# Time mixing by one level of Strassen's multiplication, with weight quarters fetched from memory

## The chip, the cores and the metric

The kernel runs on one core of one Trainium2 chip. The metric is the device time of one execution in microseconds (us). TensorE is called PE below (PEld is its weight load), VectorE DVE, ScalarE ACT, GpSimd POOL, SyncE SP. SP and ACT issue the DMA transfers.

## The reference

Four stages, each with x added back, on x of B = 128 rows, 64 channels and T = 1024 steps:

```
x1 = x  + einsum('bct,bcd->bdt', x, W[condition])         # mixes channels, weights by row
x2 = x1 + conv(x1, kernel 1), up to a length per row      # state-space filter along t
x3 = x2 + x2 @ weight.T + bias + scale * low-rank(x2)     # mixes time steps, 1024 x 1024
out = x3 + conv(x3, kernel 3), up to a length per row     # state-space filter along t
```

The third line, "time mixing", is what the change is about: `base = einsum('bsi,oi->bso', x, weight) + bias`, and `delta`, through 16 ranks of the row's adapter. It is applied to each channel's time axis.

## The kernel before

Time is cut in NBLK = 8 blocks of 128 steps, which lie on the partitions; channels in NG = 16 groups of HG = 4. Products in 16-bit are made from two halves: a value is split in a high part (rounded to f16, by ACT) and a low part (the rest, by DVE), and three matmuls (high x high, high x low, low x high) take the place of one. So `x2_split_hi` (L1017) and `x2_split_lo` (L1477) make x2h and x2l, and likewise for x1 (L1013, L1465), the state-space tables (`table_hi` L1031, `table_lo` L1444), their bases (`bases_hi` L1048, `bases_lo` L1450) and x3.

Stage 0 (`stage0`) loads x, mixes channels on PE (L618), and writes x1 to memory as `x1_scratch`. Beside it the time-mixing weights are turned on PE (`turn_lot`, 8 transposes for each of 8 output blocks) and split into `w2t`, which holds them all; `lot_ready` on DVE prepares each row block and adds the identity for the residual. Small tables go to memory with `store_tab`, filters with `store_k`.

Then PE runs `body(g)` for each group: `stage2(g)`, the time mixing of the group's 4 channels at once (512 columns); then, in an order written out by hand, the filter before the mixing for the next group (`states(0, g+1, k)`, `near1`, `far1`) and the filter behind it for this one (`states(1, g, k)`, `near3`, `far3`; L784 and L797). `stage2` begins with the low-rank sums (L737) into bank 7, then for each output block o makes 24 matmuls (L745) and 3 for the low-rank term (`delta`, L753):

```python
for k in range(NBLK):
    for q, (part, xx) in enumerate(products):
        nc.tensor.matmul(ps[:, 4 + o % 3, :], w2t[:, o, part, k, :], xx[:, :, k, :], ...)
```

DVE scales the low-rank sums (L1499) and ACT and DVE split them (L1072, L1502). As each block o ends, ACT makes its x3 high part straight from the bank (L1079), DVE reads the bank again (L1515) and makes the low part (L1509); between blocks both handle the bases and tables. After stage 2 they split the states (`state_hi` L1055, `state_lo` L1457), select the first filter's sums (`take_conv1`, L1472) and split x2.

The output of channel h goes from the banks to `outt[:, h]` (ACT, L1110, counted by c3_out). SP turns x3 (`turn_x3`, L418), POOL adds its two parts (L531, past_summed) and scales them (L534, past_ready) in `past_of`; DVE selects between the two (L1557, c3_past); SP stores it (L448, out_stored). Behind each select DVE makes a low part of x1 for the group after the next (L1465). POOL also makes the tables (`make_tables`, L507 to L521, 7 operations, twice a group): it starts them when the group's four selects are done.

All engines run their own instructions in order and wait for each other's semaphores (`wait_ge`).

## Time and profile before

| | |
|---|---|
| runs before | 1693.88, 1693.52, 1689.08 us; median 1693.52 |
| the profiled execution | 1686.25 us |
| its span, first to last instruction | 1684.4 us |
| mean granted PE clock | 0.978 of full |
| PE, DVE, ACT, POOL busy | 93%, 61%, 31%, 49% |

The rows below are from the profiled execution, times in us unless marked ns, counted from the start of its span. "Idle before" names what ended the idle time. Matmuls overlap, so a matmul's own length (379 ns for 512 columns) is more than the distance to the next one; the chain of waits shows the distances. The granted clock is 1.00 at 2.4 GHz and 0.50 at 1.2 GHz.

### The profile page before, as it was taken

What the parts mean: (1) busy time and instruction counts of PE and PEld (TensorE: products, weight loads), DVE (VectorE), ACT (ScalarE), POOL (GpSimd) and SP (SyncE); (2) the same over time, 40 slices, a digit from 0 to 9 for tenths busy, and PEclk for the clock granted to TensorE, in tenths of its full rate; (3) what the DMA queues carried; (4) which work ended last, traced back from release to release, by engine and by line L of the source; (5) the groups of instructions that cost most, each with busy time, mean ns of one, the idle gap of its engine ahead of it and who ended that gap; (6) DMA issues with size and microseconds to landing.
All of it is one profiled execution on the core that took longest, in us unless ns stands there. A gap on an engine that the chain in (4) does not pass through costs nothing.

```text
span 1684.4 us, 30702 instructions
## 1 busy us (share of the span) xinstructions
PE 1572.3 (93%) x12183; PEld 1028.3 (61%) x12183; DVE 1033.4 (61%) x1345; ACT 528.5 (31%) x674; POOL 822.0 (49%) x365
## 2 busy tenths in 40 slices
PE   6777767999999999999999999999999999999996
PEld 6776654474747475656566665656574747474744
DVE  7787775656575656565655565656566665656532
ACT  4444431332323232232323232323232323232211
POOL 2000032438292928384746556555556574738434
PEclk9989879999999999999999999999999999999998
DMA  7799957253534444352526253535352626262314
GB/s 226 270 353 338 359 206 198 44 129 83 100 102 93 107 87 122 72 137 59 150 47 158 52 141 68 137 72 137 67 142 52 147 52 142 67 142 62 83 47 100
DMA packets 425956, 216.82 MB, mean 129 GB/s; under 512 B 337144, under 2 KB 412416, under 8 KB 423872
## 3 DMA queue, kind: packets, MB, share of 16 engines
q1 hardware_dynamic: 409728, 176.67, 42.1%
q10 hardware_dynamic: 16192, 39.67, 6.4%
q8 instruction: 23, 0.38, 0.1%
q14 instruction: 13, 0.11, 0.0%
HBM read 94.19 MB, written 71.76 MB: 99 GB/s over the span
## 4 chain that ended last, share of the span: by engine, by line
PE 83%; DVE 7%; DMA 6%; issue 3%; ACT 1%; POOL 0%; POOLq 0%; DVEq 0%; SPq 0%; ACTq 0%
PE ps L745 39%; PE ps L784 7%; PE ps L675 7%; DMA arena<-in_x_dram 5%; PE ps L710 5%; PE ps L737 5%; PE ps L753 5%; PE ps L797 4%; PE ps L679 3%; PE ps L618 3%; PE ps L727 2%; PE ps L723 1%; PE ps L565 1%; DVE arena L1355 1%; DVE arena L1509 1%
## 5 line engine op out<-in xcount | busy, mean ns | idle before, releaser
L745 PE MATMUL ps<-arena,w2t 128*128 128x512 f16 x3072 | 681.3, 379 | 0.0
L745 PEld LDWEIGHTS ps<-arena,w2t 128*128 128x128 f16 x3072 | 300.4, 98 | 362.3
L531 POOL TENSOR_TENSOR arena<-arena 128x1024 f32<-128x1024 f16 x64 | 150.8, 2356 | 551.7 <-DMA arena<-arena 534.0
L1515 DVE TENSOR_SCALAR arena<-ps,biasx 128x512 f32<-128x512 f32 x128 | 94.4, 748 | 204.0 <-ACT arena L1079 203.8
L1079 ACT ACTIVATE arena<-ps,biasx 128x512 f16<-128x512 f32 x128 | 87.1, 687 | 421.1 <-PE ps L753 421.1
L507 POOL TENSOR_TENSOR arena<-arena 128x1024 f32<-128x1024 f32 x32 | 73.0, 2280 | 288.4 <-DMA arena<-tab_scratch 226.4
L618 PE MATMUL ps<-arena 128*128 128x128 f32 x1024 | 145.3, 305 | 49.1 <-DMA arena<-in_x_dram 27.1
L618 PEld LDWEIGHTS ps<-arena 128*128 128x128 f32 x1024 | 136.8, 217 | 55.4 <-issue 24.3
L710 PE MATMUL ps<-arena 128*128 128x512 f16 (+1 forms) x768 | 138.2, 331 | 8.1 <-DVE arena L1434 8.1
L784 PE MATMUL ps<-arena 128*128 128x256 f16 (+1 forms) x1536 | 138.4, 247 | 3.2 <-DVE arena L1509 3.0
L534 POOL TENSOR_TENSOR arena<-arena,one_xs 128x1024 f32<-128x1024 f32 x64 | 135.2, 2112 | 5.0
L1509 DVE TENSOR_TENSOR arena<-arena 128x512 f16<-128x512 f32 x128 | 136.0, 1073 | 0.0
L784 PEld LDWEIGHTS ps<-arena 128*128 128x128 f16 x1536 | 124.0, 98 | 14.4 <-issue 3.5
L1557 DVE COPY_PREDICATED arena<-past,arena 128x1024 f32<-128x1024 uint8 x64 | 91.5, 1432 | 59.5 <-POOL arena L534 42.3
L710 PEld LDWEIGHTS ps<-arena 128*128 128x128 f16 x768 | 74.8, 99 | 59.3 <-issue 11.4
L1465 DVE SCALAR_TENSOR_TENSOR arena<-gbuf,arena 128x1024 f16<-128x1024 f32 x64 | 104.7, 1637 | 1.2 <-ACT arena L1013 1.2
L675 PE MATMUL ps<-arena 128*128 128x128 f16 x1152 | 88.8, 220 | 13.5 <-DVE gbuf L1457 5.1
L517 POOL TENSOR_TENSOR arena<-arena 128x1024 f32<-128x1024 f32 x32 | 99.9, 3123 | 2.5
L753 PE MATMUL ps<-gbuf,bt 128*128 128x512 f16 x384 | 101.2, 379 | 0.0
L675 PE MATMUL ps<-arena,gbuf 128*128 128x128 f16 x1152 | 88.2, 220 | 8.5 <-issue 7.0
L1457 DVE SCALAR_TENSOR_TENSOR arena<-ps,arena 128x512 f16<-128x512 f32 x48 | 33.2, 692 | 96.5 <-ACT arena L1055 96.5
L737 PE MATMUL ps<-arena,at 128*128 128x512 f16 x384 | 87.6, 385 | 4.8 <-DVE arena L1477 4.8
(213 smaller groups left out, 2156.3 us busy)
## 6 DMA issues: line engine op xcount, KB each, us to landing
arena<-in_x_dram SPq DMA_DIRECT2D x64, 512.0 KB, 8.0
out_dram<-arena SPq DMA_DIRECT2D x64, 512.0 KB, 3.0
gbuf<-x_scratch SPq DMA_DIRECT2D x120, 256.0 KB, 3.7
arena<-krow_scratch SPq DMA_DIRECT2D x32, 512.0 KB, 4.5
x_scratch<-arena ACTq DMA_DIRECT2D x14, 1024.0 KB, 9.3
x_scratch<-arena ACTq DMA_DIRECT2D x14, 896.0 KB, 8.6
arena<-tab_scratch SPq DMA_DIRECT2D x32, 200.0 KB, 2.6
w2t<-in_L_cond_weight_dram ACTq DMA_DIRECT2D x8, 512.0 KB, 3.5
```

What stands on the lines that cost most here:

```text
L517: ptt(v4, v4, m4, ALU.add).then_inc(v_made, 1)
L531: nc.gpsimd.tensor_tensor(past[:, h % 2].rearrange("p (k t) -> p k t", k=NBLK), x3t[:, h % 2, 0], x3t[:, h % 2, 1], ALU.add).then_inc(past ...
L534: nc.gpsimd.tensor_tensor(past[:, h % 2], past[:, h % 2], one_xs[:, :].to_broadcast([P, T]), ALU.mult).then_inc(past_ready, 1)
L618: mm = nc.tensor.matmul(ps[:, s, j * P:(j + 1) * P], xin[:, l % NXIN, j, odd * P:(odd + 1) * P], pick[:, l * GPAIRS + j, :], start=True, s ...
L675: mm = nc.tensor.matmul(o, ut[v][:, part, 2 * h + blk, :], xx[:, h, 2 * k + blk, :], start=(q == 0 and blk == 0), stop=(k == 0 and q == 2 ...
L710: nc.tensor.matmul(o, g1[:, h, part, d * P:(d + 1) * P], m, start=(d == 0 and q == 0), stop=False)
L737: mm = nc.tensor.matmul(ps[:, 7, :], at[:, part, k, :], xx[:, :, k, :], start=(k == 0 and q == 0), stop=(k == NBLK - 1 and q == 2))
L745: nc.tensor.matmul(ps[:, 4 + o % 3, :], w2t[:, o, part, k, :], xx[:, :, k, :], start=(k == 0 and q == 0), stop=False)
L753: mm = nc.tensor.matmul(ps[:, 4 + o % 3, :], bt[:, part, o * P:(o + 1) * P], xx, start=False, stop=(q == 2))
L784: nc.tensor.matmul(ps[:, bank, c0:c0 + n], xx[:, h, j, :], g3[:, h, part, g0:g0 + n], start=(j % 4 == 0 and xx is x3h and part == 0), stop ...
L1465: stt(x1l[:, h], x1f[:, h], XS / FS, x1h[:, h], ALU.mult, ALU.subtract).then_inc(x1_lo, 1)
L1509: tt(x3l[:, :, o, :], x3f[:, o % 2], x3h[:, :, o, :], ALU.subtract).then_inc(x3_lo, 1)
```

## The change

One level of Strassen's multiplication (in the form with 7 products and shared sums). The weight is cut in 2 x 2 quarters A, x2 in quarters by time half and channel pair: T_AT = (2, 0), (0, 0), (2, NQ), (0, NQ) lists (first channel, first time block) of the quarters that the row operations turn into T0 to T3. Seven products of half size replace eight: A11 with x2, a mixed quarter with T0, another with T1, A12 with x2, a mixed quarter with T2, another with x2, and one more with T3. Each is two blocks (p = 0, 1) of 24 matmuls of 256 columns in one bank each. Banks 4 and 6 collect A11's product, are read out to SBUF (`read_part`), go on collecting with T1 and are read again, with T2, and with T3; the sums of parts are made by DVE (`add_part`).

The three quarters kept in SBUF fill three quarters of w2t. The other four (8 halves of 512 KB) are made in stage 0 (rows mixed by POOL in `mix_rows`, 12 lots in place of 8 turned by PE, split, 8 of them written by `store_lot`), and fetched again for every group by ACT's queue (`load_w`) in three slots. All stores go through one staging tile (`stage`).

DVE makes the sums and differences of x2 in place in x1f (`t_rows`, four operations of 128x1024 fp32) and, with ACT, splits them into `tt_of`, which lies where `outt` does. The x1 loads of the next group follow the T parts, the x1 splits move from the tail into stage 2. The stage-0 loops on PE, ACT and DVE are written out instead of looped; the loads of the tables are cut in two. The diff, cut to what matters:

```diff
+        slot_c = part_of(gbuf, 36, 4, F16).rearrange("p (n s k o) -> p n s k o", n=2, s=2, k=NQ)
+        w_slot = [w2t[:, 0:2, 3], w2t[:, 2:4, 3], slot_c]
+        lowd = sb("lowd", [P, 2 * HW], F16)
+        lowdh, lowdl = lowd[:, 0:HW], lowd[:, HW:2 * HW]
...
         outt = area(96, 16).rearrange("p (h t) -> p h t", h=HG)
+        x3part = [area(12 + 2 * n, 2) if n < 2 else area(112 + 2 * (n - 2), 2) for n in range(6)]
+        tt_of = [area(96 + 4 * n, 4, F16).rearrange("p (s h k b) -> p s h k b", s=2, h=2, k=NQ) for n in range(4)]
...
+                    for n, (h0, k0) in enumerate(T_AT):
+                        sp.wait_ge(t_lo, 4 * g + n + 1)
+                        for h in (h0, h0 + 1):
+                            load_x1(g + 1, h, k0 // NQ)
...
-                for h in range(HG):
-                    if more2:
-                        sp.wait_ge(x2_lo, HG * (g + 1) + h + 1)
-                        load_x1(g + 2, h, 0)
-                    if h >= 2:
-                        sp.wait_ge(past_summed, HG * g + h - 1)
-                    if more2:
-                        load_x1(g + 2, h, 1)
-                    if h >= 2:
-                        turn_x3(g, h)
+                for h in range(2, HG):
+                    sp.wait_ge(past_summed, HG * g + h - 1)
+                    if more1:
+                        load_tab(1, g + 1, h - 2)
...
+            def mix_rows(q):
...
+                ptt(mix[:, 0], rows[:, 1, low], rows[:, 1, high], ALU.add).then_inc(w_rows, 1)
+                pool.wait_ge(w_rows, 4 * q + 3)
+                ptt(mix[:, 1], mix[:, 0], rows[:, 0, low], ALU.subtract).then_inc(w2_ready, 1)
+                pool.wait_ge(w2_turned, n + 1)
+                ptt(mix[:, 1], rows[:, 0, high], mix[:, 1], ALU.subtract).then_inc(w_rows, 1)
+                ptt(mix[:, 0], rows[:, 0, low], rows[:, 1, low], ALU.subtract).then_inc(w2_ready, 1)
...
+                def block(bank, p, weight, parts, fresh, done):
+                    for n in range(2):
+                        for k in range(NQ):
+                            for q, (part, xx) in enumerate(parts):
+                                last = k == NQ - 1 and q == 2
+                                mm = nc.tensor.matmul(ps[:, bank, n * HW:(n + 1) * HW], weight(p, n, part, k), xx[:, :, k, :],
+                                                      start=(fresh and n == 0 and k == 0 and q == 0), stop=(last and done),
+                                                      skip_group_check=True)
...
+                left_low = low_parts(lowh[:, 0:HW], lowl[:, 0:HW])
+                right_low = low_parts(lowh[:, HW:2 * HW], lowl[:, HW:2 * HW])
+                for p in range(2):
+                    block(SUM_AT[p], p, resident(0), x2_quarter(0, 0), True, False).then_inc(s2_summed, 1)
+                pe.wait_ge(t_hi, 4 * g + 1)
+                pe.wait_ge(t_lo, 4 * g + 1)
+                at_least(pe, c3_out, HG * g)
+                for p in range(2):
+                    slot_loaded(p, 0)
+                    block(MIX_AT[p], p, streamed(0), t_parts[0], True, False).then_inc(s2_summed, 1)
+                pe.wait_ge(t_hi, 4 * g + 2)
+                pe.wait_ge(t_lo, 4 * g + 2)
+                for p in range(2):
+                    slot_loaded(p, 2)
+                    pe.wait_ge(s2_read, NREAD * g + 1 + p)
+                    block(SUM_AT[p], p, streamed(2), t_parts[1], False, False).then_inc(s2_summed, 1)
...
+                pe.wait_ge(low_hi, g + 1)
+                pe.wait_ge(low_lo, g + 1)
+                for p in range(2):
+                    block(OWN_AT[p], p, resident(1), x2_quarter(0, NQ), True, False)
+                    delta(OWN_AT[p], p, 0, left_low, True).then_inc(s2_summed, 1)
+                pe.wait_ge(t_hi, 4 * g + 3)
+                pe.wait_ge(t_lo, 4 * g + 3)
+                for p in range(2):
+                    slot_loaded(p, 4)
+                    pe.wait_ge(s2_read, NREAD * g + 5 + p)
+                    block(SUM_AT[p], p, streamed(4), t_parts[2], False, False)
+                    delta(SUM_AT[p], p, NQ, right_low, False).then_inc(s2_summed, 1)
+                for p in range(2):
+                    slot_loaded(p, 6)
+                    pe.wait_ge(s2_read, NREAD * g + 3 + p)
+                    block(MIX_AT[p], p, streamed(6), x2_quarter(2, NQ), False, False)
+                    delta(MIX_AT[p], p, 0, right_low, True).then_inc(s2_summed, 1)
+                pe.wait_ge(t_hi, 4 * g + 4)
+                pe.wait_ge(t_lo, 4 * g + 4)
+                pe.wait_ge(lowd_hi, g + 1)
+                pe.wait_ge(lowd_lo, g + 1)
+                for p in range(2):
+                    pe.wait_ge(s2_out, NOUT * g + 3 + p)
+                    block(SUM_AT[p], p, resident(2), t_parts[3], False, False)
+                    delta(SUM_AT[p], p, NQ, low_parts(lowdh, lowdl), True).then_inc(s2_summed, 1)
...
+            def store_lot(n):
+                q, kind = lot_kind(n)
+                if kind < 2:
+                    act.wait_ge(w2_lo, n + 1)
+                    for a in range(2):
+                        part_at = 2 * (2 * kind + a) if kind == 0 else (4, 6)[a]
+                        act.dma_start(w_dram[part_at + q // 2, :, q % 2, :],
+                                      stage[:, a].rearrange("p s i -> p (s i)")).then_inc(w_stored, 16)
...
+            def load_w(j):
+                act.dma_start(w_slot[j % 3].rearrange("p n s k o -> p n (s k o)"), w_dram[j]).then_inc(w_loaded[j % 3], 16)
+            def t_split_hi(g, n):
+                act.wait_ge(t_made, 4 * g + (2, 3, 4, 4)[n])
+                at_least(act, out_stored[n], 16 * g)
+                nc.scalar.activation(tt_of[n][:, 0], t_region(n), ACT.Copy, scale=XS / FS).then_inc(t_hi, 1)
+            def read_part(g, p, bank, n_sum, row, slot):
+                act.wait_ge(s2_summed, NSUM * g + n_sum + p + 1)
+                for n in range(2):
+                    o = row + 2 * p + n
+                    e = nc.scalar.activation(x3part[slot + p][:, n * HW:(n + 1) * HW], ps[:, bank, n * HW:(n + 1) * HW], ACT.Identity,
+                                             bias=biasx[:, o:o + 1], scale=XS / FS)
+                e.then_inc(s2_read, 1)
...
+                at_least(act, x3_lo, NBLK * g)
+                t_split_hi(g, 2)
+                act.wait_ge(low_diff, g + 1)
+                nc.scalar.activation(lowdh, lowf.rearrange("p h b -> p (h b)")[:, 0:HW], ACT.Copy).then_inc(lowd_hi, 1)
+                read_part(g, 0, 4, 0, 0, 0)
+                read_part(g, 1, 6, 0, 0, 0)
+                t_split_hi(g, 3)
+                at_least(act, past_summed, HG * g)
+                read_part(g, 0, 5, 2, NQ, 2)
+                load_w(3)
+                read_part(g, 1, 2, 2, NQ, 2)
+                load_w(4)
...
+                read_part(g, 0, 4, 4, 0, 4)
+                load_w(5)
+                read_part(g, 1, 6, 4, 0, 4)
+                load_w(6)
...
+                if more1:
+                    bases_hi(0, g + 1)
+                split_hi3(g, 0, 0, 0, 0)
+                if more1:
+                    table_hi(0, g + 1)
+                split_hi3(g, 1, 0, 2, 1)
+                if early:
+                    store_k(NBLK - 1)
+                if more1:
+                    x1_split_hi(g + 1, 0)
+                act.wait_ge(s2_summed, NSUM * g + 9)
+                load_w(7)
+                split_hi3(g, 2, 2, NQ, 2)
+                if more1:
+                    x1_split_hi(g + 1, 1)
+                act.wait_ge(s2_summed, NSUM * g + 10)
+                if more1:
+                    load_w(2)
+                split_hi3(g, 3, 2, NQ + 2, 3)
+                if more1:
+                    x1_split_hi(g + 1, 2)
+                bases_hi(1, g)
+                act.wait_ge(s2_summed, NSUM * g + 11)
+                if more1:
+                    load_w(0)
+                split_hi3(g, 4, 2, 0, 4)
+                if more1:
+                    x1_split_hi(g + 1, 3)
+                act.wait_ge(s2_summed, NSUM * g + 12)
+                if more1:
+                    load_w(1)
+                split_hi3(g, 5, 2, 2, 5)
+                read_part(g, 0, 4, 12, NQ, 0)
+                split_hi3(g, 6, 0, NQ, 0)
+                read_part(g, 1, 6, 12, NQ, 0)
+                split_hi3(g, 7, 0, NQ + 2, 1)
+                table_hi(1, g)
...
-                    if more2:
-                        x1_split_hi(g + 2, h)
+                if more1:
+                    t_split_hi(g + 1, 0)
+                    t_split_hi(g + 1, 1)
...
+            def t_rows(g):
+                dve.wait_ge(x2_hi, HG * (g + 1))
+                dve.wait_ge(x2_lo, HG * (g + 1))
+                b12, b11, b22, b21 = [t_region(n) for n in range(4)]
+                tt(b22, b22, b12, ALU.subtract).then_inc(t_made, 1)
+                tt(b12, b12, b11, ALU.subtract).then_inc(t_made, 1)
+                dve.wait_ge(t_made, 4 * g + 2)
+                tt(b11, b22, b11, ALU.add).then_inc(t_made, 1)
+                dve.wait_ge(t_made, 4 * g + 3)
+                tt(b21, b11, b21, ALU.subtract).then_inc(t_made, 1)
+            def t_split_lo(g, n):
+                dve.wait_ge(t_hi, 4 * g + n + 1)
+                stt(tt_of[n][:, 1], t_region(n), XS / FS, tt_of[n][:, 0], ALU.mult, ALU.subtract).then_inc(t_lo, 1)
...
+                low_row = lowf.rearrange("p h b -> p (h b)")
+                tt(lowl, low_row, lowh, ALU.subtract).then_inc(low_lo, 1)
+                t_split_lo(g, 2)
+                dve.wait_ge(low_lo, g + 1)
+                tt(low_row[:, 0:HW], low_row[:, 0:HW], low_row[:, HW:2 * HW], ALU.subtract).then_inc(low_diff, 1)
+                dve.wait_ge(lowd_hi, g + 1)
+                tt(lowdl, low_row[:, 0:HW], lowdh, ALU.subtract).then_inc(lowd_lo, 1)
+                t_split_lo(g, 3)
...
+                def add_part(n, bank, slot):
+                    dve.wait_ge(s2_summed, NSUM * g + 7 + n)
+                    dve.wait_ge(s2_read, NREAD * g + 1 + n)
+                    stt(x3part[slot], ps[:, bank, :], XS / FS, x3part[slot], ALU.mult, ALU.add).then_inc(s2_out, 1)
+                def lo3(n, h0, row, slot):
+                    dve.wait_ge(x3_hi, NBLK * g + n + 1)
+                    tt(x3_quarter(x3l, h0, row), x3part[slot].rearrange("p (k h b) -> p k h b", k=2, h=2),
+                       x3_quarter(x3h, h0, row), ALU.subtract).then_inc(x3_lo, 1)
+                if more1:
+                    bases_lo(0, g + 1)
+                add_part(0, 0, 0)
+                if early:
+                    split_k(NBLK - 1)
+                if more1:
+                    table_lo(0, g + 1)
+                    turn_g1(g + 1)
+                add_part(1, 1, 1)
+                lo3(0, 0, 0, 0)
+                add_part(2, 4, 2)
+                lo3(1, 0, 2, 1)
+                if more1:
+                    x1_split_lo(g + 1, 0)
+                add_part(3, 6, 3)
+                lo3(2, 2, NQ, 2)
+                if more1:
+                    x1_split_lo(g + 1, 1)
+                bases_lo(1, g)
+                add_part(4, 5, 4)
+                lo3(3, 2, NQ + 2, 3)
+                if more1:
+                    x1_split_lo(g + 1, 2)
+                add_part(5, 2, 5)
+                lo3(4, 2, 0, 4)
+                if more1:
+                    x1_split_lo(g + 1, 3)
+                lo3(5, 2, 2, 5)
+                lo3(6, 0, NQ, 0)
+                lo3(7, 0, NQ + 2, 1)
+                table_lo(1, g)
...
+                    t_rows(g + 1)
...
-                    if more2:
-                        x1_split_lo(g + 2, h)
+                    if more1 and h == 1:
+                        t_split_lo(g + 1, 0)
+                        t_split_lo(g + 1, 1)
```

In PE's order of blocks, s2_summed counts 14 a group, s2_read 8 (reads by ACT), s2_out 6 (sums by DVE). The wait for s2_summed in ACT's list ahead of load_w(7), (2), (0) and (1) is for the block that used the slot last.

## Rows read from the trace of the kernel before

**Rows 1.** The page: busy time of each engine, its share, its instructions.

```profile
PE 1572.3 (93%) x12183; PEld 1028.3 (61%) x12183; DVE 1033.4 (61%) x1345; ACT 528.5 (31%) x674; POOL 822.0 (49%) x365
```

**Rows 2.** PE's waits, the whole run: us in total, times, longest.

```profile
PE ps L618 <- DMA arena<-in_x_dram: 27.1, 10, 4.4
```

**Rows 3.** The chain of waits from 714 to 812: start, us, what.

```profile
714.30 0.98 PE ps L797 x9
...
724.17 5.18 PE ps L737 x24
729.35 10.36 PE ps L745 x48
...
775.32 0.66 PE ps L753 x3
...
779.61 0.51 PE ps L675 x6
...
811.45 5.18 PE ps L737 x24
```

**Rows 4.** DVE in order of time: start, us, line, form, idle before it.

```profile
713.56 2.45 DVE L1477 SCALAR_TENSOR_TENSOR arena<-gbuf,arena 128x1024 f16<-128x1024 f32 x2
...
720.55 1.21 DVE L1465 SCALAR_TENSOR_TENSOR arena<-gbuf,arena 128x1024 f16<-128x1024 f32 x1
725.85 1.30 DVE L1557 COPY_PREDICATED arena<-past,arena 128x1024 f32<-128x1024 uint8 x1 [4.09 <-POOL arena L534]
...
727.05 3.14 DVE L1465 SCALAR_TENSOR_TENSOR arena<-gbuf,arena 128x1024 f16<-128x1024 f32 x1
732.18 1.30 DVE L1557 COPY_PREDICATED arena<-past,arena 128x1024 f32<-128x1024 uint8 x1 [2.00 <-POOL arena L534]
...
734.51 0.68 DVE L1499 TENSOR_TENSOR gbuf<-ps,adapter_scale 128x512 f32<-128x512 f32 x1
```

**Rows 5.** POOL in order of time, the same columns.

```profile
721.52 2.22 POOL L531 TENSOR_TENSOR arena<-arena 128x1024 f32<-128x1024 f16 x1 [16.65 <-DMA arena<-arena]
723.83 1.89 POOL L534 TENSOR_TENSOR arena<-arena,one_xs 128x1024 f32<-128x1024 f32 x1
725.89 3.21 POOL L531 TENSOR_TENSOR arena<-arena 128x1024 f32<-128x1024 f16 x1 [0.18 <-DMA arena<-arena]
729.18 2.76 POOL L534 TENSOR_TENSOR arena<-arena,one_xs 128x1024 f32<-128x1024 f32 x1
```

**Rows 6.** The page: DMA issues, KB each, median us from issue to landing.

```profile
out_dram<-arena SPq DMA_DIRECT2D x64, 512.0 KB, 3.0
...
arena<-krow_scratch SPq DMA_DIRECT2D x32, 512.0 KB, 4.5
...
w2t<-in_L_cond_weight_dram ACTq DMA_DIRECT2D x8, 512.0 KB, 3.5
```

**Rows 7.** Groups by form: line, operation, shapes, count, busy us, mean ns, idle before.

```profile
L618 PE MATMUL ps<-arena 128*128 128x128 f32 x1024 | 145.3, 305 | 49.1 <-DMA arena<-in_x_dram 27.1 <-DVE arena L1355 20.0 <-ACT arena L909 1.3
...
L1013 ACT ACTIVATE arena<-gbuf 128x1024 f16<-128x1024 f32 x64 | 66.9, 1048 | 3.2 <-DVE gbuf L1364 3.2
L513 POOL TENSOR_TENSOR arena<-arena 128x1024 f32<-128x1024 f32 x32 | 66.8, 2089 | 2.5
L1110 ACT ACTIVATE arena<-ps 128x1024 f32<-128x1024 f32 x64 | 65.5, 1023 | 62.3 <-PE ps L797 62.3
...
L1055 ACT ACTIVATE gbuf<-ps 128x512 f16<-128x512 f32 x48 | 28.7, 597 | 105.6 <-PE ps L679 86.2 <-PE ps L675 19.3
```

**Rows 8.** After an idle: busy us of five engines; clock, DMA share, GB/s.

```profile
280.00:284.00 4.00, 4.00 (x11) 1.42 (x10) 3.80 (x11) 0.00 (x0) 0.00 (x0) 0.51 1.32 225
```

**Rows 9.** PE in order of time, start of the first stage 2.

```profile
279.68 7.42 PE L737 MATMUL ps<-arena,at 128*128 128x512 f16 x24 [4.80 <-DVE arena L1477]
```

**Rows 10.** Stage 0, a stretch: busy us of PE, PEld, DVE, ACT, POOL; as rows 8.

```profile
165.00:205.00 40.00, 28.89 (x257) 27.08 (x256) 32.59 (x78) 18.55 (x32) 0.00 (x0) 0.91 0.99 362
```

331 lines of the change are left out of this document (174 added, 157 removed).

## The prediction

> **What bounds the kernel now.** I read the page first: TensorE (PE) is busy 93% of the span, so the question is which of its time goes and what could make it wait [rows 1]. The table of waits follows: PE's largest waits in the whole run lie in stage 0, on the loads of x (27.1 us) [rows 2]. Then the chain of waits over one group of four channels. There the reader is to see PE's lines follow each other from 724.17 (low-rank sums, L737, the start of stage 2) to the same line at 811.45, a period of 87.3 us, with one break: stage 2 ends at 775.98 and the next states begin at 779.61 [rows 3]. So in a group PE is the bound, and cutting its columns pays only while nothing else gets in its way. Last, the timelines of DVE, ACT and POOL around that start, because the change hangs new PE work on them [rows 4, 5].
>
> **What is saved on PE.** Stage 2 has 192 + 24 matmuls of 512 columns a group. They run at 5.18/24 = 0.216 us each, 46.6 us. Afterwards there are 7 products x 2 banks x 24 = 336 matmuls and 48 for the low-rank terms, all of 256 columns. A 256-column matmul with a weight load of its own takes 0.98/9 = 0.109 us [rows 3]: weight loads stay hidden. 384 x 0.109 = 41.9 us: **-4.7 a group**, -75 over 16.
>
> The Trainium skill speaks against it here: TensorE: Matmul & The Clock Gate, "The mechanism" in its part on packing, says that a weight load overlaps with matmuls in flight only when their row groups differ, and gives a load of 128 columns 107 ns ("LDWEIGHTS"). By an estimate from that page 384 pairs would take 83 us against 70 before, 13 us a group slower. The rows just named disagree, and I drop it.
>
> **What is put in PE's way.** I set t = 0 at the start of stage 2. PE without waits: low-rank sums to 5.2, each block of 24 matmuls 2.6, each with low-rank terms 3.3. So A11 is done at 10.4, the T0 blocks at 15.7, the T1 blocks at 20.9. The first T1 block needs bank 4 to have been read (s2_read), the second needs weight slot 0 reloaded (load_w(3)).
>
> The T operands lie in the output buffers. So T0 must wait until output h = 0 of the last group has been stored, T2 until h = 2 has. Chain for a group in mid-run:
> - DVE ends x2's low halves at -8.2 (713.56 + 2.45); the four new row operations at 1.22 each (the same shape as L1477) with hand-overs end at -3.1. The output select (L1557, 1.3) of h = 0 then ends at -1.8, that of h = 1 at -0.5 [rows 4].
> - DVE and POOL do not run two-input operations on SBUF at the same time. L1465 began at 727.05 and took 3.14 instead of the 1.21 of 720.55: it ended 1.1 after POOL's L531 did (729.10). That L531, started with L1557, took 3.21 instead of 2.22, and L534 2.76 instead of 1.89 [rows 4, 5]. So each such operation waits for the other engine's current one, about 2 us.
> - POOL adds h = 2 from -0.5 to 1.6 and scales it to 3.5. Output 0 lands 3.0 after its issue [rows 6], so at 1.3; ACT's T0 high part takes 1.05 [rows 7], to 2.4. DVE's T0 low part waits for POOL: 3.5 to 4.7. POOL's next add: to 6.8. T1 low part: to 8.0. POOL's scale: to 9.9. Selects of h = 2, 3: to 11.2 and 12.4. PE wants T0 at 10.4 and T1 at 15.7: no wait.
> - DVE scales the low-rank sums: 13.1; ACT's high part: 13.8. Output 2 has landed at 14.3, ACT's T2 high part ends at 15.3. POOL begins its tables at 12.5, one operation after the other at about 2 each (L513, 2.09) [rows 7]. Between them DVE gets in the low-rank low part (15.0), T2's low part (18.1) and low_diff (20.6). ACT: lowdh to 21.0, and only then the two halves of bank 4. By L1055 at 0.60 for 512 columns and L1110 at 1.02 for 1024 a half takes 0.38, so with overlap 0.75 [rows 7]: 21.8.
>
> PE wanted that at 15.7: **stall A, +6.1**. Both ends: with no POOL wait at all the chain ends at 13.2, A = 0; with the waits before 12.4 alone, A = 2.4; with one more POOL operation, 8. I take 6.1, since before the change too the low-rank scaling (L1499) came at 10.3, 5.2 after its sums were done [rows 4], and nothing shortens that list.
>
> **Stall B.** Behind that reading ACT has bank 6 (22.5), T3's high part (23.5), bank 5 (24.3), and then issues load_w(3). 512 KB land 3.0 us (output) to 3.5 us (w2) after issue [rows 6]: 27.5. PE, from 21.8, ends its block at 24.4: **+3.1** (2.4 to 4; without A 1.3). The other fetches have time, but for one.
>
> **Stall C.** load_w(7) is in ACT's queue behind split_hi3(1), which waits for add_part(1), which DVE does after bases_lo, table_lo and turn_g1. From 30.1 (T1 done, bank read by 30.8): bases 33.3, add_part(0) 34.0, table_hi 36.3, table_lo behind POOL 39.4, turn_g1 behind POOL 41.9, add_part(1) 42.6, x1_split_hi(0) 44.3, landed 47.7. PE wants it at 46.5: **+1.2** (0 to 3).
>
> **The end of stage 2 (D).** Before, 3.6 us lay between its last matmul and the second state [rows 3]. The new list on ACT and DVE has six partial sums, eight splits and the x1 splits that were in the tail, and has table_hi(1) and table_lo(1) after all of them; PE's second state needs the state split behind these. By the same working PE ends at 57.9, table_hi at 61.8, table_lo at 63.6, the state split at 64.3: 6.4, **+2.8** (0 to 4).
>
> **Clock.** After an idle of 4.80 us the granted clock was 0.51, the 1.2 GHz level, and 24 matmuls of L737 took 7.42 instead of 5.18 [rows 3, 8, 9]. Stall A is as long, but most of the slow block is covered by B: **+0.6** (0 to 2.2).
>
> Sum of a group: -4.7 + 6.1 + 3.1 + 1.2 + 2.8 + 0.6 = **+9.1**. It holds for groups 1 to 15: 137 us. Group 0 has no earlier output to wait for; its smaller B, C and D about use up its 4.7, so 0 (-4 to +3).
>
> **Stage 0.** The mixed quarters are written out: 8 lots x 512 KB = 4.2 MB. DMA share is 0.99 at 362 GB/s there [rows 10], so **+12** (5, if it fits into gaps, to 25, if ACT stops in store_lot or in its wait for w_stored). POOL's mixing, 16 operations of 512 elements at half of L513, 17 us, and 24 in all, are hidden: it was idle there [rows 10]. The 48 more turns on PE, at the 0.14 of stage 0's matmuls of 128 columns (L618) [rows 7] some 7 us, lie beside 27.1 us of waits for x [rows 2]; without that cover they would cost 7. DVE loses lot copies. Unrolling the loops I cost at 0 (its few branches are no wait in the table). Splitting the table loads costs four short issues on SP, which waits anyway.
>
> The 4.2 MB read per group are 12 us of transfers in 87 us, unhidden only through B and C.
>
> Sum: the profiled execution is 1686.25 (span 1684.4). 1686.3 + 137 + 12 = 1835. The three runs lie up to 7.6 above the profiled one; I add 3: **1838 us**, 8.5% slower.
>
> **The rivals.**
> 1. *The queues are on time, faster.* If POOL's operations and DVE's interleave without waiting, bank 4 is read at 13.2 and only B of 1.3 and a D of 1 stay: 16 x (-4.7 + 2.3) + 12 = -26, 1660. For it: DVE and POOL are idle for 39 and 51% of the span [rows 1]. Against: the 3.14 of L1465. It decides where that reading ends, at about 16.5: after that A with B eats the 3.9 a group that stay of 4.7 when stage 0's 12 us are taken off. Chance 0.14. The full saving, no stall at all, gives 1623: 0.04.
> 2. *Half of it.* The selects and the T0, T1 parts lock, the tables do not: A 2.4, B 2.7, C and D 0.25 each: +0.9 a group, +14 and +12: 1713. Chance 0.12. Around it lies what no measurement tells apart from no change (0.3%, about 5 us), 0.03.
> 3. *Worse.* The clock falls to its lower level after A and again after D, 2.2 us each instead of 0.6 in all, and load_w(3) and (7) land as late as the filter rows do, 4.5 us after issue [rows 6], 1.0 more each: 9.1 + 3.8 + 2.0 = +14.9 a group, 15 x 14.9 + 12 = 236: 1925. Chance 0.09. The Trainium skill (DMA: Bandwidth & Descriptors, "Latency and other measured facts") lets a memory access grow from 0.2 to 2 us at high load, by an estimate 1.8 more on B, 27 us in all; no row here shows such a fetch.
> 4. The change as forecast: 0.58, its own range 1775 to 1885 (+5 to +12 a group).
>
> Above 1890 and below 1650 I leave out some 0.07 each; the chances of faster, same and slower are 0.18, 0.03 and 0.79.
>
> **What would show it.** Period above 92 us; ahead of the fifth block of stage 2 an idle of about 6 us released by ACT (the reading of bank 4), ahead of the sixth one of 3 us released by a transfer; DVE's T low parts at 2 to 3 us in the mean instead of 1.2; stage 0 longer by 12 us; matmuls of 256 columns still 0.109 apart. It is wrong if PE has no idle at the fifth block, if the 256-column pairs take longer, or if the period is under 87.

## The result, and the profile after

The changed kernel takes 1819.4 us (median of 4 runs, 1811.7 to 1829.1) against 1691.5 (4 runs, 1689.1 to 1693.9): ratio 1.0759, 95% interval 1.0701 to 1.0817. It is 7.6% slower. 1838 was forecast, 8.5% slower. The profiled execution is the fastest of the four: 1811.72 us, span 1809.9, so 125.5 us of span are to be explained.

The page of the kernel after, the rows that answer to [rows 1], and the queue that brings instructions (packets, MB, share of 16 engines; before: 23 packets, 0.38 MB):

```profile
span 1809.9 us, 37051 instructions
PE 1550.8 (86%) x14919; PEld 1317.0 (73%) x14919; DVE 1251.2 (69%) x1465; ACT 691.9 (38%) x1022; POOL 828.5 (46%) x389
...
q8 instruction: 150, 2.46, 0.6%
```

PE does less (1550.8 us against 1572.3, and some of its time is at half speed), but its share fell from 93 to 86%: it waits. For what, the table of PE's waits in the whole run says (us in total, times, longest), to be held against [rows 2]:

```profile
PE ps L829 <- ACT arena L1218: 40.5, 15, 5.1
PE ps L806 <- issue: 34.2, 13, 2.9
PE ps L743 <- DVE gbuf L1652: 31.1, 14, 2.3
...
PE ps L743 <- DVE arena L1660: 24.1, 15, 1.7
PE ps L829 <- DMA w2t<-w_scratch: 22.5, 14, 7.6
```

L829 is the block of 24 matmuls of a product, L1218 ACT's reading of a bank, L806 the low-rank sums, the first thing in stage 2, and L743 a state. Blocks are counted in PE's order, so the fifth and the sixth are those with T1. What `load_w(j)` fetches is called quarter j below, although it is half of a mixed quarter (512 KB): quarter 3 is needed by the sixth block, quarter 7 by the twelfth. The second row was in no step of the prediction: in 13 groups PE stands still ahead of stage 2 and nothing that the profile shows holds it.

One group in mid-run, PE in order of time (start, us, form, count; idle before it and its releaser), to be held against [rows 3]. Stage 1 had ended at 770.2:

```profile
772.99 5.34 PE L806 MATMUL ps<-arena,at 128*128 128x512 f16 x24 [2.80 <-issue]
778.16 10.64 PE L829 MATMUL ps<-arena,w2t 128*128 128x256 f16 x96
791.07 4.46 PE L829 MATMUL ps<-arena,gbuf 128*128 128x256 f16 x24 [2.26 <-ACT arena L1218]
796.38 5.41 PE L829 MATMUL ps<-arena,w2t 128*128 128x256 f16 x48 [0.85 <-DMA w2t<-w_scratch]
...
824.55 0.82 PE L838 MATMUL ps<-lowd,bt 128*128 128x256 f16 x6
826.98 1.50 PE L743 MATMUL ps<-arena 128*128 128x128 f16 x24 [1.61 <-DVE arena L1660]
832.73 0.70 PE L743 MATMUL ps<-arena 128*128 128x128 f16 x6 [2.29 <-DVE gbuf L1652]
868.58 5.34 PE L806 MATMUL ps<-arena,at 128*128 128x512 f16 x24 [2.39 <-issue]
```

The reader is to see five breaks: 2.80 ahead of stage 2, 2.26 ahead of the fifth block, 0.85 ahead of the sixth, and 1.61 and 2.29 ahead of the two states at the end. From the last matmul of stage 2 (825.2) to the second state it is 7.5 us, against 3.6 before. Those 3.6 were not a break, as the prediction read [rows 3]: the chain there runs over ACT and DVE, but PE works on the first state and the filter meanwhile, and its own timeline of before has two short idles in the period of 87.3 us, 0.47 late in stage 1, which stands in both kernels, and this one:

```profile
779.61 0.51 PE L675 MATMUL ps<-arena 128*128 128x128 f16 x6 [0.35 <-DVE gbuf L1457]
```

The fifth block takes 4.46 instead of 2.62. The second row's 96 matmuls with their 96 weight loads take 0.109 each: the saving on PE is there.

The other side, DVE in the same stretch, to be held against [rows 4]:

```profile
762.14 1.23 DVE L1694 TENSOR_TENSOR gbuf<-gbuf 128x1024 f32<-128x1024 f32 x1
...
765.80 1.22 DVE L1699 TENSOR_TENSOR gbuf<-gbuf 128x1024 f32<-128x1024 f32 x1
766.95 1.30 DVE L1799 COPY_PREDICATED arena<-past,arena 128x1024 f32<-128x1024 uint8 x1
...
774.46 4.92 DVE L1703 SCALAR_TENSOR_TENSOR arena<-gbuf,arena 128x1024 f16<-128x1024 f32 x2 [4.99 <-ACT arena L1212]
...
784.53 2.81 DVE L1703 SCALAR_TENSOR_TENSOR arena<-gbuf,arena 128x1024 f16<-128x1024 f32 x1
787.27 2.57 DVE L1720 TENSOR_TENSOR gbuf<-gbuf 128x256 f32<-128x256 f32 x1
```

L1694 to L1699 make T's rows, L1799 is the output select, L1703 T's low parts, L1720 low_diff. ACT reads bank 4 from 790.19 and PE goes on at 791.07: the forecast chain, end to end.

Window by window, from and to in us: its length, busy us of PE, PEld, DVE, ACT and POOL, then the granted clock, DMA share and GB/s. First the fifth block, then the second state and what follows it:

```profile
790.90:795.50 4.60, 4.43 (x24) 3.06 (x24) 3.06 (x2) 3.24 (x8) 4.52 (x3) 0.63 1.07 264
...
832.70:836.00 3.30, 3.27 (x33) 3.28 (x34) 0.00 (x0) 0.00 (x0) 1.30 (x1) 0.53 1.02 194
```

Behind these two idles, of 2.26 and 2.29 us, the granted clock was 0.63 and 0.53 in the mean of the windows, so for part of them at the 1.2 GHz level: 1.8 us are lost on the block and 1.6 on the state. Behind the 2.80 ahead of L806 it was not: 5.34, as at full speed. The same idles do not have slow work behind them in every group. In groups 1 to 14 of this trace the idle of 2.2 to 2.3 us ahead of the second state was followed by slow matmuls in 7 groups and by none in 7, the one ahead of the fifth block in 12 of 13, and the one ahead of L806 in 1 of 13.

Where the 125.5 us lie, by the starts of the first L806 (before: L737) of the 16 groups in the traces:

| stretch | before | after | difference | forecast |
|---|---|---|---|---|
| to the first group | 279.68 | 289.56 | +9.9 | +12 |
| group 0 | 95.12 | 98.40 | +3.3 | 0 |
| 14 periods, mean | 87.30 | 95.26 | +111.5 in all | 9.1 each, +127 |
| from the last start to the end | 87.5 | 88.3 | +0.8 | +9 |

### The profile page after: what moved, and what is told of

Same layout as the page of the kernel before. It is cut to its first block, busy times and chain, and to the rows that moved or that the text cites. A ratio compares the mean times of both kernels' runs of the same rounds, so it can differ in the third digit from the quotient of the medians.

```text
span 1809.9 us, 37051 instructions
## 1 busy us (share of the span) xinstructions
PE 1550.8 (86%) x14919; PEld 1317.0 (73%) x14919; DVE 1251.2 (69%) x1465; ACT 691.9 (38%) x1022; POOL 828.5 (46%) x389
## 4 chain that ended last, share of the span: by engine, by line
PE 37%; DVE 26%; DMA 16%; issue 12%; ACT 7%; POOL 2%; ACTq 0%; DVEq 0%; SPq 0%; POOLq 0%
PE ps L829 17%; PE ps L743 7%; DMA out_dram<-arena 6%; DVE arena L1703 5%; DMA arena<-in_x_dram 5%; DMA w2t<-w_scratch 4%; DVE arena L1672 4%; PE ps L838 3%; PE ps L689 3%; PE ps L747 2%; DVE arena L1799 2%; PE ps L779 2%; DVE gbuf L1720 2%; ACT arena L1212 2%; ACT arena L1218 1%
## 5 line engine op out<-in xcount | busy, mean ns | idle before, releaser
L829 PE MATMUL ps<-arena,w2t 128*128 128x256 f16 x4608 | 527.5, 274 | 23.5 <-DMA w2t<-w_scratch 22.5
L829 PEld LDWEIGHTS ps<-arena,w2t 128*128 128x128 f16 x4608 | 451.2, 98 | 85.4 <-ACT arena L1218 10.9
L1703 DVE SCALAR_TENSOR_TENSOR arena<-gbuf,arena 128x1024 f16<-128x1024 f32 x64 | 153.3, 2414 | 85.0 <-ACT arena L1212 84.3
L1231 ACT ACTIVATE arena<-arena 128x512 f16<-128x512 f32 x128 | 80.6, 630 | 241.3 <-DVE arena L1737 240.3
L743 PE MATMUL ps<-arena 128*128 128x128 f16 x1152 | 96.0, 231 | 63.2 <-DVE gbuf L1652 31.1
L829 PE MATMUL ps<-arena,gbuf 128*128 128x256 f16 x768 | 111.2, 313 | 39.5 <-ACT arena L1218 39.5
L912 PEld LDWEIGHTS ps<-arena 128*128 128x128 f16 x1536 | 123.2, 98 | 13.3 <-issue 2.8
L1218 ACT ACTIVATE arena<-ps,biasx 128x256 f32<-128x256 f32 x256 | 103.3, 475 | 75.5 <-PE ps L829 68.2
L545 POOL TENSOR_TENSOR arena<-arena 128x1024 f32<-128x1024 f32 x32 | 61.8, 1930 | 150.7 <-DVE arena L1799 53.1
L829 PEld LDWEIGHTS ps<-arena,gbuf 128*128 128x128 f16 x768 | 84.7, 112 | 62.1 <-ACT arena L1218 38.1
L743 PEld LDWEIGHTS ps<-arena 128*128 128x128 f16 x1152 | 76.3, 104 | 71.5 <-issue 69.8
L806 PE MATMUL ps<-arena,at 128*128 128x512 f16 x384 | 90.4, 394 | 39.0 <-issue 34.2
L779 PEld LDWEIGHTS ps<-arena 128*128 128x128 f16 x768 | 75.2, 100 | 60.5 <-issue 13.0
L1325 ACT ACTIVATE arena<-ps 128x1024 f32<-128x1024 f32 x64 | 65.5, 1024 | 101.9 <-PE ps L925 101.9
```

The costliest lines, as they stand in the source:

```text
L743: mm = nc.tensor.matmul(o, ut[v][:, part, 2 * h + blk, :], xx[:, h, 2 * k + blk, :], start=(q == 0 and blk == 0), stop=(k == 0 and q == 2 ...
L779: nc.tensor.matmul(o, g1[:, h, part, d * P:(d + 1) * P], m, start=(d == 0 and q == 0), stop=False)
L806: mm = nc.tensor.matmul(ps[:, 7, :], at[:, part, k, :], xx[:, :, k, :], start=(k == 0 and q == 0), stop=(k == NBLK - 1 and q == 2))
L829: mm = nc.tensor.matmul(ps[:, bank, n * HW:(n + 1) * HW], weight(p, n, part, k), xx[:, :, k, :], start=(fresh and n == 0 and k == 0 and q ...
L912: nc.tensor.matmul(ps[:, bank, c0:c0 + n], xx[:, h, j, :], g3[:, h, part, g0:g0 + n], start=(j % 4 == 0 and xx is x3h and part == 0), stop ...
L1218: e = nc.scalar.activation(x3part[slot + p][:, n * HW:(n + 1) * HW], ps[:, bank, n * HW:(n + 1) * HW], ACT.Identity, bias=biasx[:, o:o + 1 ...
```

## The experiments

Times with no count are of one run. The mean period is that of the 14 groups after group 0 (before 87.30, after 95.26). In diffs a `-` line is the changed kernel's, or that of the version named. The kernel before, run beside them, stayed at medians of 1690.2 to 1691.7. The changed kernel's own four runs lie 17 us apart, some 1.2 us a group, so a difference of under 1 us in the mean period of two single traces is not told apart from none.

**1. The readings first.**

```diff
+                read_part(g, 0, 4, 0, 0, 0)
+                read_part(g, 1, 6, 0, 0, 0)
+                act.wait_ge(s2_summed, NSUM * g + 3)
+                load_w(3)
                 act.wait_ge(low_scaled, g + 1)
                 nc.scalar.activation(lowh..., lowf, ACT.Copy).then_inc(low_hi, 1)
                 ...
-                read_part(g, 0, 4, 0, 0, 0)
-                read_part(g, 1, 6, 0, 0, 0)
                 ...
-                load_w(3)
```

> The changed kernel, with ACT's list alone reordered: both readings of A11's banks and the issue of load_w(3) stand ahead of the low-rank high part and T2. My theory (PE waits for ACT's and DVE's lists): the idle of 2.3 us before the fifth block and the 1.8 us of half clock behind it go, load_w(3) is issued some 5 us earlier and its wait (0.85) stays under 1; about -4.5 us a group, period 96.0 to 91.5, some 1750 us. Rival (the fetched weights, as transfers, are the limit): the wait moves to the sixth block, period within 1 us of 96.0.

1803.8 us, mean period 94.65. PE no longer waits at the fifth block, the place was right; but the price was not: 1750 was expected, and only some 8 to 16 us came back, 0.6 us in the mean period. In the table of waits the quarters took over. PE's waits, and DVE at 789.18 (start, us, form, idle before it):

```profile
PE ps L829 <- DMA w2t<-w_scratch: 57.3, 25, 7.2
```

```profile
789.18 1.71 DVE L1718 TENSOR_TENSOR gbuf<-gbuf 128x512 f16<-128x512 f32 x1 [4.70 <-ACT gbuf L1256]
```

The second row holds the reason, which I took in only with experiment 9: DVE stands idle for 4.70 us, because ACT, now with two readings and a wait for PE's third sum in front, makes the high part that DVE needs (L1256) so much later.

**2. PE's loop over the groups written out.**

```diff
-            with pe.Fori(1, NG - 1) as g:
+            for g in range(1, NG - 1):
```

> The changed kernel, with PE's loop over groups 1 to 14 written out. If the 2.8 us of idle before L806 (13 times, no releaser) are the jump back of the loop, they go. My theory then: the chain to the reading of bank 4 starts in the tail, not at L806, so the wait before the fifth block takes over what went (2.3 to about 5 us) and the period falls by less than 1 us: 1810 to 1825. Rival (each idle is paid by itself): -2.8 a group, 1783 us.

1800.3 us, mean period 94.4. The idle ahead of L806 is gone in all 13 groups, so the jump back of the loop was its place. The mean period fell by 0.9, as expected; the time lies 10 us under the 1810 that was the lower end. The fifth block took the idle over:

```profile
767.25 5.34 PE L806 MATMUL ps<-arena,at 128*128 128x512 f16 x24
772.43 10.64 PE L829 MATMUL ps<-arena,w2t 128*128 128x256 f16 x96
788.21 5.28 PE L829 MATMUL ps<-arena,gbuf 128*128 128x256 f16 x24 [5.14 <-ACT arena L1218]
```

PE comes to the fifth block 2.8 us earlier against the same chain on ACT and DVE and waits 5.14 there instead of 2.26; the whole block is then at half speed.

**3. The first state's split ahead of the tables.**

```diff
-                table_hi(1, g)
                 if more1:
                     state_hi(0, g + 1, 0)
+                table_hi(1, g)
+                if more1:
                     state_hi(0, g + 1, 1)
```

and the same for the low parts on DVE.

> The changed kernel, with table_hi(1) and table_lo(1) put behind the split of the first state instead of ahead of it, nothing else. My theory (D is ACT's and DVE's backlog): the second state starts about 2.2 us sooner after stage 2 and the half clock behind the idle (1.6) mostly goes: -2.2 to -3.8 a group, 1763 to 1787 us. Rival (D is the x1 splits or the transfers): under 1 us a group.

1770.1 us, mean period 92.35. The idle ahead of the second state (31.1 us in all) and the half-speed matmuls behind it are gone, 2.9 us a group, as expected. This is the part of D that was forecast, and order alone was its cause: nothing was taken from any engine. The other part stayed: PE's wait ahead of the first state, for DVE's last x1 low part, is 24.2 us in all here against 24.1, 1.6 a group. Those low parts are what the change moved from the tail into stage 2.

**4. The three together.**

> The three edits of the last three kernels together. My theory: with the reading early there is nothing behind the jump's 2.8 us to take its place, so the sum is more than its parts: -4.5 - 2.8 - 3.8 = -11.1 a group, period about 85, 1653 us, under the kernel before. Rival (transfers or DVE's total work set the pace): not under 1710.

1734.3 us (4 runs, 1733.5 to 1734.7), ratio 1.0265 (1.0239 to 1.0292), mean period 89.87. My 1653 is missed by 81. What PE waits for is now quarter 7, whose fetch is behind DVE's list:

```profile
882.82 5.21 PE L829 MATMUL ps<-arena,w2t 128*128 128x256 f16 x24 [4.94 <-DMA w2t<-w_scratch]
```

```profile
875.96 2.42 DVE L1631 COPY arena<-arena 128x2048 f16<-128x2048 f16 x1 [2.35 <-DMA arena<-krow_scratch]
878.30 0.68 DVE L1739 SCALAR_TENSOR_TENSOR arena<-ps,arena 128x512 f32<-128x512 f32 x1
```

L1631 is turn_g1, L1739 add_part(1); ACT's split_hi3(1) follows at 879.01, and only then does load_w(7) go out, at 879.20. That is stall C in the form in which the prediction worked it out.

**5. Quarter 7 fetched before split_hi3(1); 6. turn_g1 late as well.**

```diff
+                act.wait_ge(s2_summed, NSUM * g + 9)
+                load_w(7)
                 split_hi3(g, 1, 0, 2, 1)
                 ...
-                act.wait_ge(s2_summed, NSUM * g + 9)
-                load_w(7)
```

```diff
                     table_lo(0, g + 1)
-                    turn_g1(g + 1)
                 add_part(1, 1, 1)
                 ...
                 lo3(1, 0, 2, 1)
+                if more1:
+                    turn_g1(g + 1)
```

> This is the version with the three edits together (reads of banks 4 and 6 and the fetch of quarter 3 first, PE's group loop written out, first state's split first; 1734.3 us) with one more: the fetch of quarter 7 and its wait stand in ACT's list ahead of split_hi3(1). There, PE waited 4.94 us (2.7 to 4.9) for that quarter and ran the next 24 matmuls in 5.2 instead of 2.6. Mine: both go, 7 us a group at most, but DVE's list (add_part(2), add_part(3), the x1 low parts) ends no earlier, so some 3 of them come back as a wait for DVE late in stage 2 or at the states: 4 x 15 = 60 us less, 1675 us, a period of about 86 us, with less than 20 us in all of PE waiting for quarters. Rival 1 (the quarters' landing is slow whenever they are issued, 6 us, and another fetch is late instead): PE's waits on transfers stay at 40 us or more and the time above 1710. Rival 2 (nothing comes back): 1734 - 105 = 1630.

> As the version with quarter 7 fetched early, and in DVE's list turn_g1, which waited 2.35 us for its filter rows and took 2.42, stands behind add_part(1), lo3(0), add_part(2) and lo3(1) instead of ahead of them. Mine: if DVE's list is what comes back as a wait in the last blocks of stage 2, its partial sums come some 4.8 us earlier and that wait goes; the x1 low parts come 2 to 3 us earlier too, since the wait for the rows is covered. 10 to 35 us less than the version with quarter 7 early alone: 1655 us, 2% below the kernel before the change. Rival (DVE's list is not what PE waits for by then): within 5 us of the version with quarter 7 early.

1757.3 us (4 runs; 1.0393, 1.0373 to 1.0413) and 1753.8 (5 runs; 1.0385, 1.0365 to 1.0404): both slower than the 1734.3 that they were meant to improve. The fetch comes in time, PE's waits on transfers fall from 60.2 to 37.4 us, and PE waits at the first state instead, for DVE's last x1 low part (60.0 us in all):

```profile
909.99 2.72 PE L743 MATMUL ps<-arena 128*128 128x128 f16 x24 [4.67 <-DVE arena L1662]
912.50 3.05 PE L779 MATMUL ps<-arena 128*128 128x512 f16 x12
```

From the start of L806 to the first state it is 909.99 - 855.78 = 54.2 us; with quarter 7 late it was 895.08 - 839.41 = 55.7 in the group shown. DVE's last x1 low part ends 54.3 us after the start of L806 in the mean of 14 groups with quarter 7 late, 54.5 with it early and 54.1 with turn_g1 late as well. So DVE's list ends where it ended, and PE stops wherever it has got ahead of it. The half-speed work behind the earlier stop was covered by that list; the 36 matmuls behind this later stop are not, and run for 5.4 us instead of 3.3. That the sum is worse, 1.5 us in the mean period, agrees with it. I had let some 3 of 7 us come back there; all of it did, and the slow states on top. With turn_g1 late the time is 3.5 us less and not 10 to 35: the rival of that expectation came.

**7. DVE's row operations left out.**

```diff
-                tt(b22, b22, b12, ALU.subtract).then_inc(t_made, 1)
-                ...
-                tt(b21, b11, b21, ALU.subtract).then_inc(t_made, 1)
+                nc.vector.memset(small[:, 52:53], 0.0).then_inc(t_made, 4)
```

> The changed kernel without the four row operations on x2 that make T (t_rows, 4 x 1.23 us on DVE a group); one small memset counts for them, so the T products take x2's own rows instead of their sums and differences. The selects and all that stands behind them on DVE can begin 4.9 us earlier. Mine (the chain that ends in the reading of bank 4 is what stall A is): DVE's low_diff ends some 4 us earlier, PE's idle of 2.3 us ahead of the fifth block and its half-speed block go, 4 us a group; as in the run with the reads first most of it comes back at quarter 7, whose fetch is behind DVE's list: 1780 to 1805 us. Rival (the chain hangs on the landing of output 0 at 773.35, not on DVE's rows): idle at the fifth block stays 2 us or more and the time within 8 us of 1812 to 1819.

1750.8 us, mean period 91.24: 4.0 us a group, all of what DVE no longer does but for 0.9. PE's wait on L1218 falls from 40.5 to 3.2 us and nothing takes it over (waits for quarters 23.7 against 22.5). The price was that of my chain, and the 1780 to 1805 that I expected were too high: unlike the reads first, this edit shortens DVE's list.

**8. POOL's scaling cut to 16 columns.**

```diff
-   nc.gpsimd.tensor_tensor(past[:, h % 2], past[:, h % 2], one_xs[:, :].to_broadcast([P, T]), ...
+   nc.gpsimd.tensor_tensor(past[:, h % 2, 0:16], past[:, h % 2, 0:16], one_xs[:, :].to_broadcast([P, 16]), ...
```

> The changed kernel with POOL's scaling of the past (L572, 128 x 1024, 1.9 to 2.8 us, 64 of them) cut to 16 columns, so that most of the past is left unscaled. The edit takes no work from DVE, ACT or PE. Mine (DVE's and POOL's two-input operations keep each other out, so DVE's T low parts wait for POOL's): the mean of DVE's T low parts falls from 2.41 to below 2.0 us, and the idle ahead of the fifth block from 2.3 to below 1 us; in time 5 to 25 us less, 1790 to 1812, because quarter 7 takes over as with the reads first. Rival (the T low parts are long for another reason, their shape or their strides): mean within 0.15 of 2.41 and the idle unchanged.

1781.1 us, mean period 93.40, 9 us under the lower end of what I expected. DVE's T low parts (busy us, mean ns), in the changed kernel and in this one:

```profile
L1703 DVE SCALAR_TENSOR_TENSOR arena<-gbuf,arena 128x1024 f16<-128x1024 f32 x64 | 153.3, 2414 | 85.0 <-ACT arena L1212 84.3
```

```profile
L1703 DVE SCALAR_TENSOR_TENSOR arena<-gbuf,arena 128x1024 f16<-128x1024 f32 x64 | 117.9, 1844 | 86.2 <-ACT arena L1212 85.0
```

DVE has the same instruction with the same data to move, and it is 0.57 us shorter in the mean because POOL does less. The single instructions leave no other reading. In the changed kernel POOL was in an operation at the start of 60 of the 64 low parts, and each of these ended 1.08 or 1.09 us after POOL's operation did, whatever its length; the other 4 took 1.22. A DVE row and the POOL row that it waited for (POOL's end at 786.26, DVE's at 787.34):

```profile
784.53 2.81 DVE L1703 SCALAR_TENSOR_TENSOR arena<-gbuf,arena 128x1024 f16<-128x1024 f32 x1
783.88 2.38 POOL L547 TENSOR_TENSOR arena<-arena 128x1024 f32<-128x1024 f32 x1
```

With the scaling cut, the low parts of T0 and T1 take 1.23 each and those of T2 and T3, beside POOL's tables, are unchanged. So DVE's operation waits for POOL's current one. In the group read the fifth block has no wait left; the waits for quarters rose from 22.5 to 39.1 us in all.

**9. Three more orders and places.** From the version with turn_g1 late: the scaling on ACT; then turn_g1 on ACT too; and, from the first of these, the low-rank high part back to the front.

```diff
-                    nc.gpsimd.tensor_tensor(past[:, h % 2], past[:, h % 2], one_xs..., ALU.mult).then_inc(past_ready, 1)
+                    act.wait_ge(past_summed, HG * g + h + 1)
+                    nc.scalar.activation(past[:, h % 2], past[:, h % 2], ACT.Copy, scale=1.0 / XS).then_inc(past_ready, 1)
```

> The version with turn_g1 late (1753.8 us), with POOL's scaling of the past done by ACT instead (a copy with a scale, about 1.04 us each, four a group: two ahead of the conv3 outputs, one behind each of T0's and T1's high parts). ACT is busy for 38% of the span. Mine (what PE waits for is the length of DVE's list in stage 2, and DVE waits in it for POOL's two-input operations): the T low parts of T0 and T1 and the selects lose their waits for the scaling, DVE's list ends 2 to 4 us a group earlier, and PE's wait for DVE's x1 low parts at the second state falls from 48.7 us to below 20: 30 to 50 us less, 1705 to 1725. Rival (ACT's four operations delay the reading of banks 4 and 6 or T's high parts, and the gain is taken back there): 1745 or more.

> The version with the scaling on ACT, with turn_g1 (DVE, 128 x 2048, 0.7 to 2.4 us) done by ACT as well, behind split_hi3(3). Mine: DVE's list in stage 2 is shorter by 0.7 to 2.4 us and PE's wait at the second state by as much; 10 to 25 us less than the version with only the scaling on ACT, 1690 to 1710, about level with the kernel before the change. Rival (DVE's list no longer sets the end of stage 2, or ACT's copy of about 2 us delays split_hi3(4) and the fetches behind it): within 5 us of it or slower.

1724.2 us (4 runs; 1.0194, 1.0165 to 1.0222) and 1729.7 (5 runs; 1.0236, 1.0207 to 1.0265). The first gains 30, as expected, but not by the way expected: PE's wait for DVE's x1 low parts rose from 48.7 to 69.2 us in all, where I had it fall below 20, and the waits for quarters fell from 38.4 to 6.4. turn_g1's 2.8 us less on DVE bring nothing, as the rival had it. So it was not the amount of DVE's work alone that set the end of stage 2. DVE's timeline with the scaling on ACT shows a hole in it:

```profile
848.32 0.67 DVE L1721 TENSOR_TENSOR gbuf<-ps,adapter_scale 128x512 f32<-128x512 f32 x1
853.81 1.60 DVE L1725 TENSOR_TENSOR gbuf<-gbuf 128x512 f16<-128x512 f32 x1 [4.82 <-ACT gbuf L1253]
```

It is the hole of experiment 1, made by my own edit (90.9 us in all here, 81.0 in experiment 1, 11.1 in the changed kernel). So:

```diff
                 read_part(g, 0, 4, 0, 0, 0)
-                read_part(g, 1, 6, 0, 0, 0)
-                act.wait_ge(s2_summed, NSUM * g + 3)
-                load_w(3)
                 act.wait_ge(low_scaled, g + 1)
                 nc.scalar.activation(lowh..., lowf, ACT.Copy).then_inc(low_hi, 1)
                 t_split_hi(g, 2)
+                read_part(g, 1, 6, 0, 0, 0)
+                act.wait_ge(s2_summed, NSUM * g + 3)
+                load_w(3)
```

> The version with the scaling on ACT (1724.2 us), with one order on ACT changed: the high part of the scaled low-rank sums (L1253) and T2's high part stand between the reading of bank 4 and that of bank 6, instead of behind both readings and the wait for the third sum that load_w(3) needs. There, as in the version with the reads first alone, DVE stood idle for 4.8 us (848.99 to 853.81) until ACT had run L1253. Mine (the reads-first edit gave little because it put DVE's list behind PE's third block, and DVE's list sets the end of stage 2): that idle goes, DVE's list ends 4 us earlier, PE's wait for the x1 low parts at the second state (69.2 us in all, 5.1 us in the group read) falls below 20 us and the half-speed states behind it go: 45 to 80 us less, 1645 to 1680, a period of 84 to 86.5 us and faster than the kernel before the change. Rival 1 (DVE's later waits, for POOL's tables and its partial sums, take the 4 us back): 1705 or more. Rival 2 (the later fetch of quarter 3 or the later reading of bank 6 becomes PE's wait): idle ahead of the sixth block above 2 us, 1690 or more.

1684.8 us (12 runs, 1678.6 to 1696.8), ratio 0.9963 (0.9942 to 0.9983): this order alone is worth 39 us, and the kernel ends 0.4% below the one before the change, which is no gain to speak of. The mean period is 87.04 in the profiled execution, which took 1695.0, 10 us more than the median. In the same place of its trace:

```profile
750.48 0.67 DVE L1721 TENSOR_TENSOR gbuf<-ps,adapter_scale 128x512 f32<-128x512 f32 x1
751.85 1.39 DVE L1725 TENSOR_TENSOR gbuf<-gbuf 128x512 f16<-128x512 f32 x1 [0.70 <-ACT gbuf L1250]
...
767.46 2.38 DVE L1653 SCALAR_TENSOR_TENSOR arena<-arena 128x1024 f16<-128x1024 f32 x1 [3.92 <-ACT arena L1185]
```

```profile
PE ps L740 <- DVE arena L1668: 44.2, 15, 4.3
...
PE ps L826 <- DMA w2t<-w_scratch: 13.8, 13, 2.6
```

and ACT there:

```profile
765.64 0.47 ACT L1215 ACTIVATE arena<-ps,biasx 128x256 f32<-128x256 f32 x1 [3.46 <-PE ps L826]
...
766.37 1.06 ACT L1185 ACTIVATE arena<-arena 128x1024 f16<-128x1024 f32 x1
```

The hole of 4.8 is 0.70 now, but DVE waits 3.92 a little later, where it did 0.79 before: ACT reaches the basis (L1185) behind a reading (L1215) that follows PE's sum. Over the run the hole fell from 90.9 to 13.9 us, and DVE's wait for that basis rose from 31.7 to 52.4. DVE's last x1 low part ends 51.3 us after the start of L803 in the mean, against 52.4, so of the 4 us that I expected 1.2 were left. This taking back is Rival 1 by a wait that I had not named, one for ACT. Part of it is Rival 2, which I overlooked: PE's waits for quarters rose from 6.4 to 13.8, and most of that is quarter 3 ahead of the sixth block, as here in the group that starts at 566.02:

```profile
587.05 7.08 PE L826 MATMUL ps<-arena,w2t 128*128 128x256 f16 x48 [2.59 <-DMA w2t<-w_scratch]
```

The four groups in which that wait was 1.7 us or more last 88.6 to 90.8 us and have DVE's longest waits for the basis (3.7 to 4.2); the other ten last 84.9 to 87.7.

**10. The quarters stored twice.**

```diff
+        w_again = nc.dram_tensor("w_scratch2", [2 * NQ, P, 2, 2 * NQ * P], F16).ap()
 ...
                         act.dma_start(w_dram[part_at + q // 2, :, q % 2, :],
                                       stage[:, a].rearrange("p s i -> p (s i)")).then_inc(w_stored, 16)
+                        act.dma_start(w_again[part_at + q // 2, :, q % 2, :],
+                                      stage[:, a].rearrange("p s i -> p (s i)")).then_inc(w_stored, 16)
```

> The changed kernel with each mixed quarter stored twice in stage 0, the second time to another DRAM area that nothing reads: 4.2 MB more. All results stay. Stage 0's end moved from 240.3 to 248.0 us and the first A11 block from 279.7 to 289.6 with the change. Mine (stage 0 is paced by its transfers at 362 GB/s): another 8 to 12 us, the first A11 block at 298 to 302, nothing later. Rival (the 8 to 10 us come from the mixing, the turns or the unrolled loops): below 3 us.

The counts of w_stored that ACT waits for are doubled with it, so ACT waits for the second stores too.

1824.6 us. The last matmul of stage 0, in the changed kernel and here (ns min/median/max; first and last start):

```profile
L689 PE MATMUL ps<-arena x1024: 273/275/583, 31.2 to 247.7; 128*128 128x128 f32 x171
```

```profile
L690 PE MATMUL ps<-arena x1024: 273/275/582, 31.2 to 254.8; 128*128 128x128 f32 x171
```

Before it was 240.0: the first 4.2 MB brought +7.7, the second +7.1. So the stores set stage 0's end, and they explain nearly all of it. Whether by the rate of the transfers or by ACT's waits for the staging tile this edit does not separate; those waits are 4.4 us in all in the changed kernel and 6.3 here. The first group starts at 295.2 against 289.6, +5.6, under my 8 to 12; since that start lies anywhere from 287.0 to 293.3 in the versions above, which share stage 0, I read no more into the difference between 7.1 and 5.6, nor into the 2.2 us that lie between 7.7 and the 9.9 of the first group.

## Why the prediction was right, and where its terms were not

The forecast case came: slower by stalls A to D in the order given, 8.0 us a group in the mean against 9.1. The terms, from the group read, 772.99 to 868.58 (95.6 - 87.3 = +8.3; the terms below make 8.2):

| term | forecast | measured | what the runs showed |
|---|---|---|---|
| PE's columns | -4.7 | -4.6 | 0.109 a pair; what is left of 95.6 without idle, the delay at the end and the slow blocks is about 82.7 |
| loop jump | not named | +2.4 | 2.39, the one at the end of this period; experiment 2 |
| stall A | +6.1 | +2.3 | 5.14 once PE's loop is written out |
| stall B | +3.1 | +0.85 | load_w(3) went out earlier |
| stall C | +1.2 | 0, but 7.6 in group 0 | appears when PE runs ahead of DVE (experiments 1 and 4) |
| D | +2.8 | +3.9 | 2.3 by the order (experiment 3), 1.6 ahead of the first state |
| clock | +0.6 | +3.4 | half speed after A and after D; less in the mean, as half of the groups have none after D |

**A** was right in its chain and off by what PE did ahead of it. Counted from the end of stage 1 (770.2), where PE would have started without the jump, bank 4's reading lets PE go on 20.9 us later; I had worked out 21.8. Of that, the loop jump took 2.8 and the stall 2.3, and experiment 2 turned them into one stall of 5.14. That DVE's and POOL's operations wait for each other, which stretched the chain, was read from one row of 3.14 us; experiment 8 shows it.

**B** failed on one point: I put load_w(3) behind ACT's readings and T3's high part. ACT in order of time, in the changed kernel (ACTq are transfers that it issues):

```profile
790.19 0.46 ACT L1218 ACTIVATE arena<-ps,biasx 128x256 f32<-128x256 f32 x1
790.43 0.54 ACTq L1207 DMA_DIRECT2D w2t<-w_scratch  x1
790.55 0.83 ACT L1218 ACTIVATE arena<-ps,biasx 128x256 f32<-128x256 f32 x2
...
791.62 1.07 ACT L1212 ACTIVATE arena<-gbuf 128x1024 f16<-128x1024 f32 x1
```

The fetch (L1207) goes out during the readings and ahead of T3's high part (L1212), which stands before it in the list. Counted from the end of stage 1 it went out at 20.2, not 24.3, which took 4.1 us off. It landed 5.8 us after its issue, not 3.2, which put 2.6 back. And the fifth block, at half speed, ended 0.9 later than I had it: 3.1 - 4.1 + 2.6 - 0.9 = 0.7, near the 0.85 measured. The Trainium skill's remark on latency under load (DMA: Bandwidth & Descriptors, "Latency and other measured facts"), with which I had priced a rival at 1.8 us, points the right way: the median landing of the quarters in w2t was 4.7 us, 6.0 in the version with the three edits, against 3.0 to 3.5 in [rows 6]; whether memory or the queues take the time no run here tells.

**C** was worked out against a PE that A lets start early; PE came later and it vanished. It was real all the same: in experiments 1 and 4, with A gone, PE waited for quarter 7, 1.6 to 4.9 us in most groups. In experiment 7, where A goes because DVE's list is shorter, it came in group 0 alone.

**D** was mis-sized by 1.1. The chain to the second state was the forecast one (table, split, second state), but 1.6 of its 3.9 us PE already waits at the first state, for x1's low parts, which the prediction lists as moved and does not price; putting the split first leaves that part. The recorded sum has a slip here too: from 47.7 three blocks of 3.3 end at 57.5, not 57.9, which makes D 3.2 by its own working and the group 9.5. And its 3.6 us of before are work on PE with 0.35 of idle, not a break.

**The clock** was under-priced. I let B cover A's slow block, but B was short, and I had no slow block after D. The worse rival had 2.2 for each; 1.8 and 1.6 were measured in the group read, the second in half of the groups only.

**Stage 0** at +12 was the transfer time at the full rate; 7.7 to 9.9 were measured. Part of the bytes fits into gaps, as my lower end of 5 allowed for: from 60 to 160 us the rate was 344 GB/s before and 361 after, and behind that, to the end of stage 0, 324 and 346.

So the sum is near by luck in good part: three errors below (jump, D, clock: 6.3 us a group) and three above (A, B, C: 7.3) offset each other, and 2 us of stage 0 lie above as well. A and the jump are partly one error, as the jump was taken out of A's stall. What was right is that the stalls outweigh the columns saved, and where three of the four lie. The Trainium skill's rule on weight loads (TensorE: Matmul & The Clock Gate, "The mechanism"), by which 13 us a group would have been added by my estimate, did not hold here: 96 loads of full 128x128 weights stay hidden behind 96 matmuls of 256 columns, 0.109 us a pair.

What the prediction did not see is what the stalls have in common. Stages 1 and 2 hang on one list on DVE, with ACT's beside it, and PE meets it at four places. Taking work off that list, or waits for POOL out of it (experiments 7 and 8), gave 1.9 to 4.0 us a group; letting PE run ahead of it gave 0.6 to 0.9 (1 and 2), which the spread of the runs does not tell from nothing, or made it worse (5). My first edit had put a hole in that list, and the versions built on it kept it. That the hole was worth 39 us is shown by the swap of experiment 9 alone; what the 4.3 us are made of by which the last version's period still exceeds PE's own 82.7 is only read from its table of waits (2.9 at the state, 0.9 on quarters, the rest slow matmuls). Group 0 takes 101 to 105 us in the versions with the readings first, against 98.4. In experiment 1 the trace has the same hole there, 8.30 us on DVE, and behind it a wait on PE that the changed kernel does not have, 4.64 us for DVE's filter tables, with the next block at 4.17 us instead of 2.79; no run takes this hole out alone.

## What to carry to other kernels

When work is taken from the bound engine and fed by the others, write out the other engines' lists between two of its meeting points first, with their waits; their length is what the period cannot go below, and a stall removed at one meeting point returns at the next until the list itself is shorter. In a list in program order look for waits on the bound engine: each operation behind one becomes as late as that engine, and moving something important ahead of it can pull everything else behind it. Half-speed work behind a stall costs nothing while the bound engine has still to wait for the others' list, and is paid in full behind the last such wait. In the changed kernel's group from 1536.89 the low-rank sums ran at half speed for 8.1 us instead of 5.2; the stall at the fifth block was gone in return, and the group took 92.8 us, less than any before it.

## What was not expected of the hardware

- PE lost 2.3 to 2.9 us at the jump of its loop over the groups in 13 groups, 34.2 us in all; the loop of the kernel before, with fewer instructions (12183 matmuls in the run against 14919), lost none that its table shows. Written out, it was gone, and the queue of instructions brought 119 packets instead of 150. That the jump waits for instructions to be brought is my reading of these two numbers, not shown.
- ACT's transfers went out ahead of copies that stand before them in its list: the fetch at 790.43, T3's high part, which stands ahead of it, at 791.62.
- Idles of 2.26 and 2.29 us had half-speed matmuls behind them (4.46 us instead of 2.62, at a granted clock of 0.63), the idle of 2.80 at the jump had not; and the same idle of 2.2 us ahead of the second state had them in 7 groups of 14. What makes the difference no run here tells. A price for such an idle is a chance, not a sum.
- DVE's T low parts (both inputs in SBUF) that started while POOL was in a two-input operation ended 1.08 or 1.09 us after POOL's did, 60 times of 60 in the changed kernel; where POOL was idle they took 1.22 to 1.23 us.
